# Recurrence steps dealt out unequally over the units, splits of states and additions put in other gaps

## The reference

```python
xn = _layernorm(x)
x = x + _L0_attn_ref(xn, ...) + _L0_ffn_ref(xn, ...)      # linear attention, 8 heads of 32; 16 experts, top 6, 176 wide
xn = _layernorm(x)
x = x + _L1_attn_ref(xn, ...) + _L1_ffn_ref(xn, ...)      # recurrence; 8 experts, top 2, and 2 shared ones

def _L1_attn_ref(x, W_in, b_in, W_out, b_out, gamma, beta):
    u = jnp.einsum('bsd,hd->bsh', x, W_in) + b_in         # hidden size 512
    def step(state, u_t):
        s = jnp.tanh(u_t + state * gamma + beta)
        return (s, s)
    _, states = jax.lax.scan(step, init, jnp.swapaxes(u, 0, 1))
    return jnp.einsum('bsh,dh->bsd', jnp.swapaxes(states, 0, 1), W_out) + b_out
```

## Time and profile before

| | us |
|---|---|
| median of 3 runs | 668.85 (666.12 to 669.87) |
| the profiled execution | 664.72 |
| its span | 663.1 |
| PE busy | 615.1 (93%) |
| DVE busy | 446.1 (67%) |
| ACT busy | 366.4 (55%) |
| POOL busy | 240.0 (36%) |

### The profile page before, as it was taken

The page is one execution under the profiler, slowest core; times in us unless marked ns, Lnnn a source line. Parts: engine busy times, 40 slices in busy tenths (PEclk is TensorE's granted clock), DMA queues, the critical chain, the costliest instruction groups (busy, mean ns, idle before and its releaser), DMA issues. The chain is left out here.

```text
span 663.1 us, 12527 instructions
## 1 busy us (share of the span) xinstructions
PE 615.1 (93%) x3579; PEld 339.9 (51%) x3579; DVE 446.1 (67%) x1525; ACT 366.4 (55%) x1004; POOL 240.0 (36%) x256
## 2 busy tenths in 40 slices
PE   6999899999999989999999988999967999978897
PEld 2665344544444434444454434454544667646675
DVE  7874877657863676685487696467686565676675
ACT  3445454456536456556756656745646765664551
POOL 4246222122242225523224524122542172464372
PEclk9999999999999999999999999999987999989999
DMA  8104577773396354845435650405411344753233
GB/s 297 77 1 138 189 245 254 245 231 96 107 343 216 117 167 137 268 143 181 160 129 198 225 186 1 187 32 90 94 49 41 89 144 114 161 151 110 74 115 108
DMA packets 89531, 97.99 MB, mean 148 GB/s; under 512 B 29358, under 2 KB 80142, under 8 KB 89038
## 3 DMA queue, kind: packets, MB, share of 16 engines
q10 hardware_dynamic: 45328, 45.88, 21.2%
q1 hardware_dynamic: 38862, 36.95, 19.0%
q0 software_dynamic: 5280, 14.42, 7.0%
HBM read 27.96 MB, written 63.24 MB: 138 GB/s over the span
## 5 line engine op out<-in xcount | busy, mean ns | idle before, releaser
L1927 POOL TENSOR_TENSOR hl<-scr,hh 128x512 f16<-128x512 f32 (+2 forms) x91 | 105.4, 1158 | 280.2 <-ACT hh L1300 280.2
L1332 ACT ACTIVATE RING<-zbuf 128x16 f32<-128x16 f32 x512 | 111.0, 217 | 145.7 <-DVE zbuf L1774 141.1
L746 PE MATMUL G<-xT,W 128*128 128x512 f16 (+2 forms) x600 | 145.9, 379 | 5.1 <-ACT scr L1292 2.6
L746 PE MATMUL U<-xT,W 128*128 128x512 f16 (+2 forms) x600 | 145.8, 379 | 2.3 <-DVE scr L1789 2.3
L746 PE MATMUL Y<-hh,W 128*128 128x512 f16 x352 | 119.2, 379 | 6.6 <-POOL hl L1927 6.5
L1774 DVE TENSOR_TENSOR_SCAN zbuf<-C,RING 128x32 f32<-128x32 f32 x339 | 74.3, 219 | 73.9 <-ACT RING L1332 73.5
L746 PEld LDWEIGHTS U<-xT,W 128*128 128x128 f16 (+3 forms) x600 | 60.9, 102 | 71.3 <-DVE scr L1789 3.6
L746 PEld LDWEIGHTS G<-xT,W 128*128 128x128 f16 (+3 forms) x600 | 60.2, 102 | 69.6 <-issue 5.4
L1292 ACT ACTIVATE scr<-G 128x512 f32<-128x512 f32 (+2 forms) x100 | 58.9, 589 | 54.4 <-PE G L746 53.3
L1795 DVE TENSOR_TENSOR U<-U,CS 128x512 f32<-128x512 f32 x88 | 60.3, 685 | 38.7 <-PE U L746 32.2
L1300 ACT ACTIVATE hh<-scr 128x512 f16<-128x512 f32 (+2 forms) x100 | 61.8, 618 | 26.3 <-DVE scr L1789 26.2
(11 more groups left out here) (196 smaller groups left out, 841.9 us busy)
## 6 DMA issues: line engine op xcount, KB each, us to landing
xrows<-zeros ACTq DMA_DIRECT2D x13, 1280.0 KB, 5.9
yrows<-zeros ACTq DMA_DIRECT2D x10, 1536.0 KB, 6.0
stage<-weights SPq DMA_DIRECT2D x20, 384.0 KB
yrows<-zeros ACTq DMA_DIRECT2D x5, 1408.0 KB, 6.1
yrows<-scr POOLq DMA_DIRECT2D x46, 128.0 KB
xrows<-zeros ACTq DMA_DIRECT2D x5, 1152.0 KB, 5.3
stage<-weights SPq DMA_DIRECT2D x14, 256.0 KB
parked<-RING SPq DMA_DIRECT2D x1, 3520.0 KB, 12.8
```

Source lines behind the costliest of these rows:

```text
L746: last = nc.tensor.matmul(bank_, w(wp), act(ap), start=start and n == 0, stop=stop and n == count - 1)
L1332: nc.scalar.activation(RING[:, (t + 1) % RING_T, ::2], zbuf[:, 1::2], ACT.Tanh).then_inc(state_done, 1)
L1927: nc.gpsimd.tensor_tensor(hl[rows, a, :], h32[a][rows, :], hh[rows, a, :], ALU.subtract)\
```

## The change

It has four parts, none of which changes what is computed:

- UNIT_STEPS becomes a list with a number for each unit: 6 in units 0 to 2, 4 in 3 to 5, 6 in 6 to 8, 8 in 9 to 13, 7 in 14 to 17, 6 in 18 to 31, 0 in 32 to 34. The sum is still 200; the last step is in unit 31. Gaps 0 to 5 exist in each unit, with or without a step. Gamma is read from PSUM in units 30 and 31 too, and the wait for block 3's inputs (more_inputs) moves from unit 10 to unit 12.
- Splits of block 0: one each in front of pairs 9 and 10 of phase 2 and pairs 2 and 3 of phase 3. Of block 1: one each in front of pairs 9 and 10 of phase 3, and the other two with their heads in gap 5 of units 0 and 1 and their tails in gap 1 of units 1 and 2. Of block 2: units 15 to 18, head in gap 4, tail in gap 5. Of block 3: two in each of units 32 and 33.
- Additions of units 19 to 26: one in gap 1 and one in gap 5, no longer both at the end. The gathers stay where they are.

```diff
-UNIT_STEPS = {"S": SLOTTED, "R": SLOTTED + 1}
+UNIT_STEPS = (6, 6, 6, 4, 4, 4, 6, 6, 6, 8, 8, 8, 8, 8, 7, 7, 7, 7, 6, 6, 6, 6, 6, 6, 6, 6, 6, 6, 6, 6, 6, 6, 0, 0, 0)
...
-        UNITS_HELD = (0, 1, 2, 28, 29)
+        UNITS_HELD = (0, 1, 2, 28, 29, 30, 31)
...
-        FIRST_SPLIT, FIRST_ATTEND = (2, 2, 3, 3), 8
+        FIRST_SPLIT, FIRST_ATTEND = ((2, 9), (2, 10), (3, 2), (3, 3)), 8
...
+            for c, (at, k) in enumerate(FIRST_SPLIT):
+                if at == phase:
+                    front[k].append(("split_states", (0, c)))
             if phase == BLOCKS - 1:
-                for c in range(KH):
-                    front[FIRST_SPLIT[c]].append(("split_states", (0, c)))
                 front[FIRST_ATTEND].append(("attend", (0, other)))
+                for c in range(2):
+                    front[FIRST_ATTEND + 1 + c].append(("split_states", (1, c)))
...
-            10: [("more_inputs", (4,)), ("scatter", (3, 0)), ("scatter", (3, 1))],
+            10: [("scatter", (3, 0)), ("scatter", (3, 1))],
             11: [("scatter", (3, 2)), ("scatter", (3, 3))],
+            12: [("more_inputs", (4,))],
...
         GATHERS = {**{18 + n: (2 * n, 2 * n + 2) for n in range(8)}, 29: (16, 32)}
-        COMBINES = {**{19 + n: (2 * n, 2 * n + 2) for n in range(8)}, 31: (16, 20), 32: (20, 24), 33: (24, 28)}
+        COMBINES = {31: (16, 20), 32: (20, 24), 33: (24, 28)}
...
-                     **{(1 + c, 3): ("states_head", (1, c)) for c in range(KH)},
-                     **{(1 + c, 5): ("states_tail", (1, c)) for c in range(KH)},
...
+                     (0, 5): ("states_head", (1, 2)), (1, 1): ("states_tail", (1, 2)),
+                     (1, 5): ("states_head", (1, 3)), (2, 1): ("states_tail", (1, 3)),
+                     **{(19 + n, 1): ("combine", (2 * n,)) for n in range(8)},
+                     **{(19 + n, 5): ("combine", (2 * n + 1,)) for n in range(8)},
+                     **{(15 + c, 4): ("states_head", (2, c)) for c in range(KH)},
+                     **{(15 + c, 5): ("states_tail", (2, c)) for c in range(KH)},
...
             def unit_step(u, i):
-                state_at(steps_to(u) + i)
+                if i < UNIT_STEPS[u]:
+                    state_at(steps_to(u) + i)
                 unit_gap(u, i, gaps)
```

More of the change, by code:

```diff
@@ L82 @@
          + [("S", j, g) for j in (1, 2, 3) for g in range(3)])
+UNIT_STEPS = (6, 6, 6, 4, 4, 4, 6, 6, 6, 8, 8, 8, 8, 8, 7, 7, 7, 7, 6, 6, 6, 6, 6, 6, 6, 6, 6, 6, 6, 6, 6, 6, 0, 0, 0)
+assert len(UNIT_STEPS) == len(UNITS)
 DENSE0 = BLOCKS * CH0
@@ L438, in build @@
                      (8, 0): ("input_copy", (3, 2, Y[1][0])), (8, 2): ("input_copy", (3, 3, Y[1][1])),
-                     **{(1 + c, 3): ("states_head", (1, c)) for c in range(KH)},
-                     **{(1 + c, 5): ("states_tail", (1, c)) for c in range(KH)},
-                     **{(20 + c, 3): ("states_head", (2, c)) for c in range(KH)},
-                     **{(20 + c, 5): ("states_tail", (2, c)) for c in range(KH)},
-                     **{(30 + c, 2): ("states_head", (3, c)) for c in range(KH)},
-                     **{(30 + c, 4): ("states_tail", (3, c)) for c in range(KH)}}
+                     (0, 5): ("states_head", (1, 2)), (1, 1): ("states_tail", (1, 2)),
[4 more added lines that the diff above has]
+                     **{(15 + c, 5): ("states_tail", (2, c)) for c in range(KH)},
+                     (32, 0): ("states_head", (3, 0)), (32, 2): ("states_tail", (3, 0)),
+                     (32, 3): ("states_head", (3, 1)), (32, 4): ("states_tail", (3, 1)),
+                     (33, 0): ("states_head", (3, 2)), (33, 2): ("states_tail", (3, 2)),
+                     (33, 3): ("states_head", (3, 3)), (33, 4): ("states_tail", (3, 3))}
         COMBINED_BEFORE = (0, 16, 28)
@@ L503, in steps_to @@
         def steps_to(u):
-            return STEPS * TICKS0 + sum(UNIT_STEPS[UNITS[m][0]] for m in range(u))
+            return STEPS * TICKS0 + sum(UNIT_STEPS[:u])
         def group_of_pair(r):
@@ L1381, in _ @@
                     unit_step(u, 4)
-                for i in range(5, UNIT_STEPS[kind(n)]):
+                for i in range(5, max(SLOTTED, UNIT_STEPS[u])):
                     unit_step(u, i)
@@ L1842, in unit_step @@
                 def unit_step(i):
-                    scan_at(steps_to(u) + i, u in UNITS_HELD)
+                    if i < UNIT_STEPS[u]:
+                        scan_at(steps_to(u) + i, u in UNITS_HELD)
                     if u in UNIT_WOVEN and i < SLOTTED:
@@ L1847, in unit_step @@
                             share[name](block_, first + each * i + part)
-                    unit_gap(u, i, {"states_tail": split_states})
+                    unit_gap(u, i, {"states_tail": split_states, "combine": combine})
                 unit_front(u, share)
```

## The result

| | before | changed |
|---|---|---|
| median of 13 runs, us | 668.66 | 670.02 |
| ratio to before, 95% interval | 1 | 1.0034 (1.0021 to 1.0047) |
| the profiled execution, us | 664.72 | 670.85 |
| its span, us | 663.1 | 669.2 |

The changed kernel is slower by 0.34%, 2.3 us, or by 1.4 us if the medians are subtracted. The interval leaves out 1, but either number is inside the half per cent that was named as telling nothing. The forecast was 672.0, and the measured 670.0 is at the lower edge of its 670 to 674.

The account below looks back on a forecast made before the run. It took PE to bound the dense pairs and the DVE scan and ACT tanh chain the units. Eight terms summed to +3.15 us: 667.9 in the profile's execution, 672.0 beside the median (forecast 670 to 674, full range 666 to 676.5).

Parts of the forecast that it names:

- Term 1: Block 0's splits into phase 2 pairs 9 and 10: PE loses 3.7 us there, wins 1.0 at phase 3 pair 3.
- Term 2: Block 1's splits into phase 3 pairs 9 and 10, where PE has less slack: +2.7 us (1.5 to 3.5).
- Rival (a): Dense pairs hide the moved splits of blocks 0 and 1: 1 us in place of 6.4, 666.6 us; chance 0.20.
- (c): Split tails moved into dense pairs lose the shared port to POOL, 0.76 us each: +6.2, 675.0 us; chance 0.20.
- Term 5: Block 2's splits in units 15 to 18: units 15 to 17 take 1.45 us more each, +4.35 us (3.5 to 5).
- term 7: Units 25 and 26: one step and the additions less at unit 25's end, PE's G waits less: -0.9 us.
- term 8: The end: DVE overloaded in units 32 and 33 by splits and additions, attend(3) and store later: +1.4 us (0 to 2.5).
- Term 4: Eight steps in units 9 to 13, chain-bound, 0.51 us per added step where not hidden: +1.8 us (1.0 to 2.6).
- Term 3: Fewer steps in units 3 to 8, with splits gone from the early units: -6.1 us (-4 to -8).
- Term 6: Units 18 to 23: splits gone, six steps, additions in gaps 1 and 5 that wait for gathers: -2.8 us.
- rival (b): Gathers do not hold the additions, units 19 to 23 take 3.5 us each, 7 less: 664.8 us; chance 0.12.
- The step to the median: Whole kernel: the median of three runs lay 4.1 us above the profiled execution; the same was added to both kernels.

Follow-up runs that it names:

- control: The changed kernel timed and profiled once more with no edit, against the kernel before: ratio 1.0026 (1.0007 to 1.0046), span 667.4 us.
- steps back: Changed kernel with 7 steps again in units 3 to 17 and the wait for block 3's inputs in unit 10: 1.0049 of the kernel before.

## Why the prediction came out as it did

**The bound** was read rightly: a full PE in the dense pairs, the chain of scan and tanh in the units. (PE's 3.55 us for a unit leave out its last matmul: by the earlier trace rows it is 3.71, 531.56 to 534.89 + 0.38. No term hangs on it.)

**Terms 1 and 2.** Each place and each wait was as described. Term 1 was +2.95 for +2.7: 3.9 in phase 2 (3.7 forecast) and -0.95 at pair 3 (-1.0). Term 2 was +2.1 in PE's waits and +3.35 at unit 0's first scan, for +2.7. Rival (a), that the pairs hide the splits, is out, and so is (c): the four tails that moved into dense pairs took 1.02 to 1.04 us each, with nothing of the 1.78 of the earlier trace rows. The rule on the shared port in the Trainium skill, "SBUF — State Buffer", section "Terms", was thus not put to the test.

**Term 5** (+4.23 for +4.35), **term 7** (-1.00 for -0.9) and **term 8** (+1.55 for +1.4) held by the marks, 5 and 8 with an experiment each. **Term 4** was +1.31 for +1.8.

**Term 3** came out at -5.98 for -6.1, but by luck: its range held in one profile of the changed kernel and not in the other. It is a sum of three parts (the forecast's first is what its sum leaves for these units):

| units | forecast | first profile | control |
|---|---|---|---|
| 0 to 2 | -0.8 | -1.4 | -1.4 |
| 3 to 5 | -3.8 | -5.6 | -5.6 |
| 6 to 8 | -1.5 | +1.0 | -1.5 |
| sum | -6.1 | -6.0 | -8.5 |

Units 3 to 5 gained 1.8 us more than forecast, and the lower clock in units 6 and 7 of the first profile took 2.5 back. At a full clock the term is -8.5, outside its -4 to -8 (before had the lower clock from 504.9 to 511.7 itself, which may be a part of that). Its sizes were off in both directions: steps back showed 0.36 us for a step in units 3 to 5, not 0.51, and the splits that left units 1 to 4 were worth more (4.2 us, with the clock's doubt).

**Term 6** was mis-sized too: -1.28 for -2.8. Its mechanism was right, and unit 18 (4.74 for 4.8), 19 (5.35 for 5.1) and 20 (4.95 for 4.6) came close; 21 and 22 were 4.72 and 5.33 for 5.3 and 4.4. What failed is "it lands 3.2 us after issue" as a constant: in the changed kernel the five that DVE waited for in units 19 to 23 started their additions 3.33, 3.51, 2.88, 3.21 and 4.68 us after the issue, and unit 23 took 6.14 in place of 5.5. That additions one unit later save 7.6 us in these five units shows what the loop costs: rival (b)'s 7 us were the right price for a change that wasn't made.

The Trainium skill, "Perfetto Trace Analysis", section "DMA Instruction — SWDGE (GPSIMD)", says that the end of such an instruction in the profile is the end of making descriptors, and that the movement of the data isn't in it. The trace agrees: the row of the gather at 598.88 lasts 1.01 us, and its addition could start 4.26 us after its start.

**The step to the median failed.** I added the same 4.1 us to both kernels. The profiled execution of the changed kernel came out 0.8 us over its median, that of before 3.9 under. So the forecast for the profile, 667.9, was 3 us too low (670.85), and that for the median, 672.0, 2 too high: the terms were too small by 2.0 us, most of it terms 2 and 6, another 1.0 came before anything is changed, and the 4.1 us on top were 4.9 too many. (By the control's marks the eight are +2.9, +3.3, -8.5, +1.3, +4.2, -1.1, +0.5 and +1.55, +4.2 in all, the +0.5 with the lower clock in unit 24.) That the range held the time owes something to two errors of opposite sign.

The granted clock of each execution shows a part of what a typical execution of before has more than the profiled one. The profile of before has a mean granted clock of 0.986. Of the 31 executions of before beside the control (a 32nd took 2250 us) only six have that, with 665.2 to 666.3 us; the middle one has 0.981, and the twelve with 0.979 or less took 668.1 to 671.7. The changed kernel has 0.992 and 0.989 in the middle of its two sets of executions, and 0.987 in its profile. So the profile of before is one of its quick executions, and the change seems to spare some of the lower clock that before typically has, which no term had. Where in the program, no run here shows: before was not profiled again. A half clock in units 6 and 7 can't be all of it, as the profile of before has a granted clock of 0.50 from 504.9 to 511.7 already.

## What to carry to other kernels

Work moved under a full engine is paid at once and in full, and only the difference to what it costs where it stood is a gain; here one of two such moves paid (block 1's splits, by 0.9 us; block 0's lost 3). Before a consumer of a DMA is moved up in its program, add up the whole loop from the copy that feeds the store to the consumer: if it is longer than the distance, the wait lands in the chain, and moving the consumer down by one stage may be worth more than all the balancing around it. A single profile can lie several microseconds off the median, and not alike for two kernels. So compare its granted clock with that of the other executions, and compare stretch by stretch between marks with the same clock: a term that comes out as forecast can be two errors.
